# A 16-stream audio tower on one core: signal loads split by rows, interpolation on VectorE alone, the position softmax moved into the first experts, and the first column halves built by rows and then turned

## The reference, cut to what matters

```
x: (16, 4096) float32
h = tok(x)       # 4x cubic interpolation, windows of 64 with step 64 (255 per stream),
                 # kw = 0.5*(w+1.3)^2 + 0.5*exp(-0.5*(w-0.7)^2), M = |fft(kw)| over 64,
                 # Mt = M*sigmoid(M - 0.12*max M), out = softmin(Mt, 0.9*max M)  -> (16, 255, 64)
h = h + attn0(layernorm(h))        # 8 heads, softmax, values from x itself
h = h + ffn0(layernorm(h))         # 16 experts, top 2, then its own layernorm, gamma, beta
h = h + attn1(layernorm(h))        # patch softmax mixed with a position softmax by a gate:
                                   # pos = softmax_k(wpos0*d + wpos2*d*d + bpos), d = k - q, per head
h = h + ffn1(layernorm(h))         # 8 experts, top 2
```

## Time and profile before

| what | value |
|---|---|
| runs | 911.83, 909.3, 911.78 us |
| profiled execution: its own time, its span | 908.39 us, 906.5 us |
| granted clock of TensorE, mean | 0.904 |
| busy: PE, PEld, DVE, ACT, POOL | 76%, 41%, 71%, 54%, 38% |
| moved by DMA | 24.31 MB, mean 27 GB/s |
| ends of the phases, from the rows of the trace | tokens 98, prep0 126, attention0 378, experts0 574, prep1 607 us |

### The profile page before, as it was taken

The page is one execution under the profiler, slowest core; times in us unless marked ns, Lnnn a source line. Parts: engine busy times, 40 slices in busy tenths (PEclk is TensorE's granted clock), DMA queues, the critical chain, the costliest instruction groups (busy, mean ns, idle before and its releaser), DMA issues. The chain is left out here.

```text
span 906.5 us, 16572 instructions
## 1 busy us (share of the span) xinstructions
PE 686.8 (76%) x5035; PEld 375.4 (41%) x5035; DVE 642.9 (71%) x1681; ACT 490.5 (54%) x1237; POOL 342.4 (38%) x374
## 2 busy tenths in 40 slices
PE   0003146899999999579999996568999999966995
PEld 0002124566666666323333322444555555556332
DVE  0299856988889889357788886746788888836343
ACT  0035446877677766245666664525666666622532
POOL 0299343577686776511122112442232222230000
PEclk9997557999999999889999998777999999965898
DMA  0200200000000000132323331000000000000000
GB/s 9 82 0 0 92 1 0 2 1 0 0 0 1 0 0 1 69 95 95 97 95 107 108 110 52 1 2 1 2 1 0 0 0 0 0 1 0 7 21 20
DMA packets 21241, 24.31 MB, mean 27 GB/s; under 512 B 11854, under 2 KB 12110, under 8 KB 20942
## 3 DMA queue, kind: packets, MB, share of 16 engines
q1 hardware_dynamic: 18989, 23.31, 8.3%
q10 hardware_dynamic: 2209, 0.49, 0.3%
HBM read 22.48 MB, written 1.31 MB: 26 GB/s over the span
## 5 line engine op out<-in xcount | busy, mean ns | idle before, releaser
L883 POOL TENSOR_TENSOR big<-big 128x1024 f32<-128x1024 f32 x64 | 120.4, 1893 | 80.7 <-DVE big L805 80.7
L734 ACT ACTIVATE big<-ps,big 128x255 f32<-128x255 f32 x256 | 117.5, 486 | 10.0 <-DVE big L799 9.5
L1720 ACT ACTIVATE big<-ps,b1s 128x512 f32<-128x512 f32 x128 | 80.5, 681 | 40.9 <-PE ps L1629 40.8
L799 DVE TENSOR_REDUCE big<-ps 128x4 f32<-128x1020 f32 x64 | 74.6, 1205 | 27.6 <-PE ps L636 27.6
L1431 DVE TENSOR_REDUCE big<-ps 128x4 f32<-128x1020 f32 x65 | 79.2, 1218 | 16.3 <-PE ps L1278 14.4
L812 DVE COPY mid<-ps 128x512 f32<-128x512 f32 x128 | 82.0, 681 | 5.7 <-DVE res L817 2.9
L1637 PE MATMUL ps<-big,w2s 128*64 128x512 f32 x256 | 69.0, 618 | 7.9 <-ACT big L1720 7.9
L1629 PE MATMUL ps<-big,wall 64*128 64x512 f32 x256 | 74.5, 650 | 0.0
L726 ACT ACTIVATE big<-ps 128x512 f32<-128x512 f32 x64 | 39.4, 616 | 64.0 <-PE ps L624 38.5
L646 PE MATMUL ps<-cst,big 128*128 128x128 f32 x512 | 71.1, 278 | 3.8 <-DVE mid L812 2.2
L1848 DVE SCALAR_TENSOR_TENSOR big<-ps,b2s,mid 128x512 f32<-128x512 f32 x64 | 48.0, 750 | 31.9 <-issue 12.0
(11 more groups left out here) (254 smaller groups left out, 1448.8 us busy)
## 6 DMA issues: line engine op xcount, KB each, us to landing
mid<-spread_w SPq DMA_DIRECT2D x128, 128.0 KB, 2.8
mid<-in_split_sel SPq DMA_DIRECT2D x1, 1536.0 KB, 6.2
wall<-in_w SPq DMA_DIRECT2D x1, 1280.0 KB, 7.1
cst<-in_consts SPq DMA_DIRECT2D x1, 666.5 KB, 5.0
mid<-in_w_raw SPq DMA_DIRECT2D x1, 620.0 KB, 6.3
w2s<-in_w SPq DMA_DIRECT2D x1, 512.0 KB, 3.2
out_tokens<-res SPq DMA_DIRECT2D x8, 64.0 KB
out_tokens<-res SPq DMA_DIRECT2D x8, 63.5 KB
```

What stands on the lines that cost most here:

```text
L734: last = nc.scalar.activation(e_sb[r % 4][:, jj, tq, 0:NW], S[:, 2 * (r % 2) + jj, tq, 0:NW], ACT.Exp, scale=-1.0, bias=minus[r % 4][:, jj ...
L799: nc.vector.tensor_reduce(minus[r % 4], S[:, 2 * a:2 * a + 2, :, 0:NW], AX.X, ALU.min).then_inc(s_mx, 1)
L883: nc.gpsimd.tensor_tensor(e_sb[r % 4], e_sb[r % 4], bc(inverse[r % 4].unsqueeze(3), [P, 2, 2, 256]), ALU.mult).then_inc(s_A, 1)
L1720: last = nc.scalar.activation(hid[e % 2][j], H1(e, j), ACT.Relu, bias=b1s[0][:, 2 * e + j:2 * e + j + 1])
```

## The change

- Signal loads: each 127-partition load becomes one of 112 and one of 15 partitions. The taps go first on ACT's queue, the raw weights before the constants and the position weights on SP's. VectorE waits for the loads of tile 0 (and the taps), and for those of tile 1 only before tile 1.
- Interpolation: VectorE does it all, in three stages (tile 0, then each half of tile 1), with the kernel function, the weights' rest and the power sums placed between taps. ScalarE does the casts of the weight split. TensorE has a PSUM bank for each group. Four scalings are folded into `scalar_tensor_tensor`; the absolute value moves from ScalarE to VectorE.
- Position softmax: the scores leave `tokens`, maxima and exps leave `attention0`. In `experts0`, POOL makes a head's scores per chunk, a chunk ahead (two in chunk 0), VectorE takes the maximum in slot 3, ScalarE the exps after slot 7.
- `attention_prep0`: `RowParts` splits the normalised rows into bf16 parts before they are turned; TensorE then turns bf16 (8 per chunk), and VectorE copies the columns out of PSUM.
- Stores of `experts1`: each of the two becomes 112 rows and the rest (16 or 15).

```diff
-                    sp.dma_start(sig[1:P, 0], bass.AP(tensor=t0, offset=HOP - 2,
-                                                      ap=[[HOP, P - 1], [SIG, B], [1, REACH]])).then_inc(s_sig, 16)
+                    sp.dma_start(sig[1:113, 0], windows(1, 112)).then_inc(s_sig[0], 16)
+                    sp.dma_start(sig[113:P, 0], windows(113, P - 113)).then_inc(s_sig[0], 16)
...
+                    act.dma_start(tw, taps).then_inc(s_tw, 16)
+                    act.dma_start(sig[0:112, 1], windows(P, 112)).then_inc(s_sig[1], 16)
+                    act.dma_start(sig[112:P - 1, 1], windows(P + 112, P - 113)).then_inc(s_sig[1], 16)
...
+            STAGES = ((0, 0, B), (1, 0, B // 2), (1, B // 2, B // 2))
...
+                    nc.scalar.activation(hi, raw, ACT.Copy).then_inc(s_hi, 1)
+                    window_parts(0)
+                    act.wait_ge(s_rest, 1)
+                    nc.scalar.activation(md, raw_rest, ACT.Copy).then_inc(s_md, 1)
+                    nc.scalar.activation(lo[D:P], raw[D:P], ACT.Copy).then_inc(s_md, 1)
+                    window_parts(1)
+                    for g in (0, 1):
+                        turned_out(g)
+                    for g in (0, 1):
+                        squares(g)
+                    window_parts(2)
+                    for g in (2, 3):
+                        turned_out(g)
+                        squares(g)
...
+                    for k in (1, 2, 3, 4, 0):
+                        tap(*STAGES[0], k)
+                    dve.wait_ge(s_sig[1], 16 * 3)
+                    for k in (1, 2):
+                        tap(*STAGES[1], k)
+                    dve.wait_ge(s_hi, 1)
+                    nc.vector.tensor_tensor(raw_rest, raw, hi, ALU.subtract).then_inc(s_rest, 1)
+                    kernelled(0)
+                    for k in (3, 4, 0):
+                        tap(*STAGES[1], k)
+                    for k in (1, 2):
+                        tap(*STAGES[2], k)
+                    dve.wait_ge(s_md, 1)
                     link(nc.vector.tensor_tensor(lo[0:D], raw_rest[0:D], md[0:D], ALU.subtract))
+                    kernelled(1)
+                    for k in (3, 4, 0):
+                        tap(*STAGES[2], k)
+                    power_sum(0)
+                    kernelled(2)
+                    power_sum(1)
...
-                    interpolate(nc.gpsimd, link, 1, 0, B - 6).then_inc(s_z[1], 1)
...
+            def high(self, act, c, tiles):
+                nc.scalar.activation(self.ra[:, c, :, 0], tiles, ACT.Copy).then_inc(self.s_hi, 1)
+                nc.scalar.activation(self.rb[:, c, :, 0], tiles, ACT.Copy).then_inc(self.s_h2, 1)
...
+                for k, rows in enumerate((self.ra, self.rb)):
+                    for t in range(TC):
+                        last = nc.tensor.transpose(self.turned[:, c % self.RING, k, P * t:P * t + P],
+                                                   rows[:, c, t].rearrange("p a d -> p (a d)"), ident_b[:])
...
+                    for c in range(CH + 3):
+                        if c < CH:
+                            normed(c)
+                        if 1 <= c <= CH:
+                            rows.subtract(dve, c - 1, xr[:, c - 1])
+                        if c >= 3:
+                            rows.columns_out(dve, c - 3)
...
-                            n = P - tq
+                            for first, n in ((0, 112), (112, 16 - tq)):
...
+                            if e == COLUMNS + 1:
+                                pos_exps(c)
...
-                        extra = [[first], [total, stats], [variance, second], [places], [shares, spread], [next_stats, next_variance], [gain, shift], [add]]
+                        extra = [[first], [total, stats], [variance, second], [places, lambda: pos_max(c)], [shares, spread], [next_stats, next_variance], [gain, shift], [add]]
...
+                    def pos_scores(h):
+
+                        link_p(nc.gpsimd.tensor_scalar(term, dist, posw[:, 0, h:h + 1], zb[:, h:h + 1], ALU.mult, ALU.add))
+                        link_p(nc.gpsimd.tensor_scalar(pexp[:, :, h], d2, posw[:, 2, h:h + 1], 0.0, ALU.mult, ALU.add))
+                        link_p(nc.gpsimd.tensor_tensor(pexp[:, :, h], pexp[:, :, h], term, ALU.add))
+                        nc.gpsimd.memset(pexp[:, :, h, NW:NW + 1], -1e30).then_inc(s_pos, 1)
+
                     def chunk(c):
                         if c < CH - 2:
                             fetch(c + 2)
                         if c >= 1:
                             own_root(c - 1)
+                        for h in ((0, 1), (2,), (3,), (4,), (5,), (6,), (7,), ())[c]:
+                            pos_scores(h)
                         if c >= 2:
                             next_root(c - 2)
```

More of the change, by code:

```diff
@@ L179, in tokens @@
             low = spec(4)
[L180 to L188, removed]
@@ L200, in interpolate @@
[L200 to L216, removed]
@@ L285, in _ @@
                     nc.vector.memset(small[:, 2:3], 1.0).then_inc(s_sm, 1)
-                    dve.wait_ge(s_sig, 16 * 4)
+                    dve.wait_ge(s_sig[0], 16 * 3)
+                    dve.wait_ge(s_tw, 16)
                     link(nc.vector.tensor_copy(sig[0:1, 0, :, 0:2], bc(sig[0:1, 0, :, 2:3], [1, B, 2])))
[L289 to L294, removed]
@@ L309, in _ @@
                         link(nc.vector.tensor_reduce(top[:, t], mag[:, t], AX.X, ALU.max))
-                        link(nc.vector.tensor_scalar(thr[:, t], top[:, t], -ALPHA, None, ALU.mult))
-                        nc.vector.tensor_tensor(arg[:, t], mag[:, t], over(thr, t), ALU.add).then_inc(s_arg, 1)
-                    link(nc.vector.tensor_scalar(cap, top, BETA, None, ALU.mult))
+                        nc.vector.scalar_tensor_tensor(out=arg[:, t], in0=over(t), scalar=-ALPHA, in1=mag[:, t], op0=ALU.mult, op1=ALU.add).then_inc(s_arg, 1)
                     for t in (0, 1):
@@ new lines, in transform @@
+                    def transform(g):
+                        pe.wait_ge(s_kT, g + 1)
+                        for c in range(4):
+                            last = nc.tensor.matmul(ps[:, 4 + g, P * c:P * c + P], kT[:, g, P * c:P * c + P], dft, start=True, stop=True)
+                        last.then_inc(s_ft, 1)
+                    pe.wait_ge(s_cst, 16)
+                    pe.wait_ge(s_kw, 1)
+                    turn(0)
+                    turn(1)
+                    transform(0)
+                    transform(1)
@@ L375, in tower @@
+                    for g in (2, 3):
+                        pe.wait_ge(s_kw, g)
+                        turn(g)
+                        transform(g)
         class ColumnParts:
@@ L417, in attention_prep0 @@
             xc = mid[:, 2048:4096].rearrange("p (t d) -> p t d", t=NT)
-            s_xc, s_sq, s_var, s_sd, s_x2 = (sem(f"a0_{n}") for n in ("centred", "squared", "var", "sd", "normed"))
+            xr = big[:, 0:2048].rearrange("p (c t d) -> p c t d", c=CH, t=TC)
+            half_rows = lambda n: big[:, 2048 * n:2048 * n + 2048].bitcast(BF16).rearrange("p (c t a d) -> p c t a d", c=CH, t=TC, a=2)
+            rest = big[:, 6144:8192].rearrange("p (c t d) -> p c t d", c=CH, t=TC)
+            turned = ps[:, 0:4].bitcast(BF16).rearrange("p i (k q) -> p i k q", k=2)
+            s_xc, s_sq, s_var, s_sd, s_x = (sem(f"a0_{n}") for n in ("centred", "squared", "var", "sd", "normed"))
             s_w, s_b2 = sem("a0_weights_in"), sem("a0_output_biases_in")
-            cols = ColumnParts("a0", *columns, copy_on_dve=True)
+            rows = RowParts("a0", half_rows(1), half_rows(2), rest, turned)
             half = NT // 2
@@ L462, in _ @@
                         if c < CH:
-                            cols.high(act, c)
+                            act.wait_ge(s_x, c + 1)
+                            rows.high(act, c, xr[:, c])
                         if c >= 1:
-                            cols.middle(act, c - 1)
+                            rows.middle(act, c - 1)
                 @block.tensor
@@ L469, in _ @@
                     for c in range(CH):
-                        pe.wait_ge(s_x2, c // 2 + 1)
-                        cols.turn(pe, c)
+                        rows.turn(pe, c)
                 @block.gpsimd
@@ L485, in _ @@
                     for c in range(CH):
-                        cols.low(pool, c)
+                        rows.low(pool, c)
                 @block.sync
@@ L1710, in next_scale, with pos_exps @@
                                                  scale=norm.rs[:, t:t + 1], bias=norm.shift[:, t:t + 1]).then_inc(s_nx, 1)
+                    def pos_exps(h):
+                        act.wait_ge(s_pmax, h + 1)
+                        for tq in range(2):
+                            nc.scalar.activation(pexp[:, tq, h], pexp[:, tq, h], ACT.Exp, bias=pmax[:, tq, h:h + 1],
+                                                 accum_out=psum[:, tq, h:h + 1]).then_inc(s_pexp, 1)
                     def chunk(c, q):
```

217 lines of the change are left out of this document (115 added, 102 removed).

## The result

The changed kernel takes 879.73 us (median; 879.5 to 880.11), the kernel before 911.45 beside it: a ratio of 0.966, 95% interval 0.964 to 0.967. The prediction was 872, range 862 to 886. The profiled execution took 879.5 us, span 877.1.

A forecast was written before the change was run, and what follows sets the result against it. Bound first by VectorE's 34.7 us signal wait, then VectorE's pace to 98 us, with TensorE busy 19.68 of 21 us per `experts0` chunk. Terms -42.5 - 1 - 3.5 + 12.5 - 3 = -37.5 gave 870.9, plus 1: 872 us, range 862 to 886.

The forecast's parts named there:

- Loads: Start of the kernel: signal on 16 engines, last byte there at 5.5 us, in place of VectorE's 34.7 us wait.
- S: VectorE's start after the signal and taps have loaded, taken as 6.5 us, bounds 5.5 and 10.
- the rival in which 112 rows still go through one engine: Signal loads: the split does nothing, S stays near 36, gain shrinks by 29.5, total 901 us; chance 0.04.
- VectorE in tokens: Interpolation from S, products at lone prices, done at S + 26.3; tokens end at 55.5 us, -42.5 us.
- The serial end: End of tokens, from the last square through roots, maxima, sums, masks, exp and logs: 15.0 us.
- Prep0: `attention_prep0`: 2.0 to 2.5 us per chunk, phase 25 to 29 us against 26.7; -1 us, bounds -3 and +3.
- Attention0: `attention0` without VectorE's maxima and ScalarE's exps: -3.5 us, bounds -1.5 and -4.5, some of the difference being TensorE's clock.
- Experts0: `experts0`: maximum (0.9) and POOL contention (1.15) delay the combined weights, 1.95 us in chunks 1 to 6; +12.5, bounds +5, +18.
- the rival on the slower side: `experts0`: TensorE's clock falls, chunks run at 1.2 GHz, 1018 us, or 945 for half of them; chance 0.02.
- POOL locks VectorE out: `experts0`: VectorE operations on two SBUF tensors wait out whole POOL instructions, 16.5 us more, 888 us; chance 0.12.
- The additions hide: `experts0`: added work fits VectorE's 3.4 us of idle per chunk, costing +3, total 862 us; chance 0.12.
- Stores: Final stores at the kernel's end, in four issues: they end at 901.0, last data at 902.0; -3 us, bounds -2 and -3.6.

The follow-up runs named there:

- the best one: Changed kernel with POOL's scores ahead of `own_root` and the maximum of heads 1 to 7 in slot 0, head 0's in slot 5: 859.32 us, ratio 0.943.

## Why the prediction was right, and where it was off

Its direction and its range held; its centre was 7.7 us too low. That the range held is in part luck: `experts0`, at +22.5, is outside its own bounds (+5 to +18), and `attention_prep0` and `attention0` made up 3.7 us of it.

- *Loads, right.* VectorE starts at 6.85 against S = 6.5. The old split puts back 29.9 us of span, so the rival in which 112 rows still go through one engine is refuted.
- *VectorE in tokens, right in kind, small terms too low.* The 1024-wide products take 1.23 us. The small ones take 0.61 (256 wide) and 0.39 (128) us where I had 0.47 and 0.32 from a slope; they work on every fourth column, and a 256-wide product over neighbouring columns takes 0.42 in `attention_prep0`. The last square ends at S + 35.3, not S + 33.5. The serial end took 14.7 us against 15.0, and from the last VectorE row to the next phase it is 1.5 us. -40.7 for -42.5.
- *Prep0.* Of the two prices of the copy the lower held: 0.41 us for one, 0.375 of busy time (6.0 / 16), against 0.42. The sum was loose: eight chunks of 2.0 to 2.5 us, 8.4 and 4.5 are 29 to 33 us, not 25 to 29. It came near because the first chunk's way (4.0 us) covers work of the next ones: 8.6 to the first norm, 4.0 to the first copy, 11.4 for all copies, 0.8 to the end. -2.8 for -1, inside its bounds, and shown by putting the old phase back.
- *Attention0.* -5.4 for -3.5, outside the bounds (-1.5 to -4.5). The stretch of slots 1 to 5 alone gained 5.0; I had read it off three later slots (28.1 us for four), but without the maxima these early ones take 27.0. The part that I gave to the clock is not there, as its rise shows.
- *Experts0, the term that was wrong.* The pause per chunk was nearly as forecast, 1.64 against 1.95 us: 0.8 for the maximum, 0.84 for the contention, where I had 0.9 and 1.15. What was left out of the sum is the clock. I had it only in the rival on the slower side, which "decides once VectorE's chain grows by about 3 us", and priced it as whole chunks at 1.2 GHz. It fell with a chain longer by 1.64 us, and in some chunks with one longer by 0.8 to 0.9, and its price is one short stretch in a chunk: 11.0 us, not 74. The kernel before with two added maxima shows that the pause alone does it: 1.85 us, 0.92, 21.8 us. So the pauses are some 11.8 us, near the +12.5 forecast (chunk 0 took 0.8 + 1.2 for 0.9), and the 11.0 of the clock stood nowhere in the sum.
- *POOL locks VectorE out, in part.* The sum over a chunk was under half of what that rival says, but single instructions do wait for the end of POOL's, as L1831 and the 1.12 us for four columns show. The maximum and the products that read PSUM did not, so the sum stayed small. 0.34 us per microsecond was a mean over a stretch with other neighbours.
- *The additions hide, possible but not as written.* Placed by VectorE's idle time they hide all but 2.2 us (slot 0); in slot 3 nothing is hidden.
- *Stores, right.* -3.05 for the phases behind `experts0`, 2.9 of it seen in the trace with the old stores.

## What to carry to other kernels

When an added instruction makes a nearly always busy TensorE wait, price the wait twice: its length, and the matmuls behind it at half the clock; here each was about half of the loss. Place such work by the engine's idle time and its readers' order, not by its own earliest moment: with the scores early, the same maximum costs 3.7 us more in slot 5 than in slot 0, 6.5 more in slot 3 and 40.5 more in slot 6. Of the 20 us between the changed kernel and the best one, 14 came with the scores' place alone.

## What was not expected of the hardware

- TensorE's granted clock fell from 2.4 to 1.2 GHz after a pause of 1.85 us (with one of 1.11 us shortly before it) in a stage where the kernel before kept it busy for 98.64 of 105.21 us, and was back after 3.4 us. With pauses of 0.2 us for the weights and none above 1.2 elsewhere it never fell in these chunks (the kernel before, and the maximum in slot 5 or 0 with the scores early); with 1.01 and 1.13 it fell in two chunks, with 1.64 to 1.85 in four to six.
- A VectorE instruction on four columns of SBUF took 1.12 us beside a POOL tensor_tensor of 1.79, against 0.17 alone, and ended 0.03 us behind it. Beside POOL's scores a reduction over SBUF (0.69) and a product that reads PSUM (0.75) took no longer than without them.
- POOL's three score operations took 0.81, 0.69 and 1.28 us here, 1.14, about 1.0 and 1.76 in tokens, where VectorE worked on 496 to 1240 columns at a time beside them: both sides of such a pair are longer.
